# The last stage of a fused layer: u evicted bank by bank, products moved ahead of the LoRA and gate steps, result stored in quarters

## The reference, cut to what matters

```python
x = x + s4_conv(paged_attention(x))          # the convolution runs along the 512 features
X = x                                        # "x1" in the kernel
z = X @ W2.T + b2 + 2.0 * (X @ lA[ids]) @ lB[ids].T              # cond2: linear plus LoRA
result = z @ W.T + b                                             # the last layer
q, k = z @ Wq.T, z @ Wk.T                                        # 8 experts of 32
w = softmax(sum(q * k over the 32) / sqrt(32))                   # the gate
combined = sum_e w[e] * (z @ A[e].T) @ Bm[e].T
out = X + result + combined
```

## Time and profile before

| | |
|---|---|
| median of 3 runs | 1333.55 us (1330.68 to 1333.7) |
| the profiled execution | 1330.66 us |
| its span | 1328.8 us |
| PE busy | 1252.7 us, 94% |
| mean granted TensorE clock | 0.976 |
| last stage of half 0, from the end of `Wo` to the next half | 606.3 to 679.3 us of the span |
| last stage of half 1, from the end of `Wo` to the end | 1256.4 to 1328.8 us of the span |

### The profile page before, as it was taken

The page is one execution under the profiler, slowest core; times in us unless marked ns, Lnnn a source line. Parts: engine busy times, 40 slices in busy tenths (PEclk is TensorE's granted clock), DMA queues, the critical chain, the costliest instruction groups (busy, mean ns, idle before and its releaser), DMA issues.

```text
span 1328.8 us, 28755 instructions
## 1 busy us (share of the span) xinstructions
PE 1252.7 (94%) x7378; PEld 1044.1 (79%) x7378; DVE 812.1 (61%) x1724; ACT 810.9 (61%) x2256; POOL 768.2 (58%) x901
## 2 busy tenths in 40 slices
PE   6899969999999998998989999699999999999998
PEld 4678859989999986765657788598989899978756
DVE  5976546776767666852147766376776767665412
ACT  3676658888888873431135766478888888744320
POOL 3444348888888864533033434388888888754310
PEclk9999979999999998998989999799999999999999
DMA  7241388888888825305134322888888888234200
GB/s 242 88 135 63 123 235 221 234 244 241 233 229 237 233 64 171 124 1 191 37 108 127 114 93 87 243 226 236 239 241 231 234 233 236 76 114 151 101 0 32
DMA packets 148104, 214.82 MB, mean 162 GB/s; under 512 B 25844, under 2 KB 120374, under 8 KB 142006
## 3 DMA queue, kind: packets, MB, share of 16 engines
q1 hardware_dynamic: 128646, 202.75, 52.3%
q10 hardware_dynamic: 18576, 9.05, 2.5%
q0 software_dynamic: 800, 2.10, 0.5%
HBM read 203.33 MB, written 10.49 MB: 161 GB/s over the span
## 4 chain that ended last, share of the span: by engine, by line
PE 81%; DVE 6%; issue 3%; DMA 3%; ACT 3%; ACTq 2%; POOL 1%; SPq 0%; DVEq 0%; POOLq 0%; PEldq 0%
PE PS L1031 17%; PE PS L999 9%; PE PS L930 4%; PE PS L926 4%; PE PS L922 4%; PE PS L1040 4%; PE PS L1090 3%; PE PS L1081 3%; PE PS L1087 3%; PE PS L966 2%; PE PS L968 2%; PE PS L1139 2%; PE PS L901 2%; PE PS L984 2%; PE PS L988 2%
## 5 line engine op out<-in xcount | busy, mean ns | idle before, releaser
L574 POOL TENSOR_TENSOR kv_parts<-kv,k_hi 128x544 fp32r<-128x544 f32 x192 | 258.6, 1347 | 41.7 <-ACT k_hi L765 40.2
L1031 PE MATMUL PS<-probT,kv 128*128 128x128 f32 x2048 | 270.5, 275 | 0.0
L527 POOL TENSOR_TENSOR ring_parts<-ring,kv_parts 128x512 fp32r<-128x512 f32 x96 | 128.9, 1349 | 229.8 <-ACT kv_parts L641 229.8
L1031 PEld LDWEIGHTS PS<-probT,kv 128*128 128x128 f32 x2048 | 249.0, 192 | 0.1
L1461 DVE COPY probT<-PS 128x512 f32<-128x512 f32 x256 | 175.6, 686 | 3.1 <-PE PS L999 3.1
L804 ACT ACTIVATE ring<-ring,smin 128x544 f32<-128x544 f32 x192 | 143.8, 749 | 37.8 <-DVE smin L1455 36.8
L1455 DVE CUSTOM_DVE_ANT_0 ring<-PS,mask,rq 128x544 f32<-128x544 f32 x192 | 150.1, 782 | 21.8 <-PE PS L989 13.5
L765 ACT ACTIVATE k_hi<-kv 128x544 fp32r<-128x544 f32 x192 | 126.0, 657 | 52.6 <-PE PS L989 48.7
L605 POOL TENSOR_TENSOR ring_parts<-ring,kv_parts 128x512 fp32r<-128x512 f32 x64 | 89.3, 1400 | 104.5 <-ACT kv_parts L844 104.4
L562 POOL TENSOR_SCALAR ring<-ring,rinv 128x512 f32<-128x512 f32 x192 | 133.3, 694 | 0.0
L922 PE MATMUL PS<-kv_parts 128*128 128x512 f32 x384 | 115.1, 417 | 18.4 <-ACT kv_parts L641 15.7
(11 more groups left out here) (212 smaller groups left out, 2711.2 us busy)
## 6 DMA issues: line engine op xcount, KB each, us to landing
kv<-in_kpages SPq DMA_DIRECT2D x512, 128.0 KB, 2.3
kv<-in_vpages SPq DMA_DIRECT2D x496, 128.0 KB, 3.2
ring<-in_w SPq DMA_DIRECT2D x46, 1024.0 KB, 4.9
kv<-in_xT SPq DMA_DIRECT2D x4, 1024.0 KB, 8.8
v_new<-kv ACTq DMA_DIRECT2D x64, 64.0 KB, 2.9
k_new<-kv ACTq DMA_DIRECT2D x16, 256.0 KB, 2.3
kv<-k_new SPq DMA_DIRECT2D x32, 128.0 KB, 2.6
kv<-v_new SPq DMA_DIRECT2D x32, 128.0 KB, 2.4
```

Of the source, the lines that this page charges most:

```text
L574: nc.gpsimd.tensor_tensor(kbuf_lo(par)[:, :, g, :], kbuf(par)[:, :, g, :], k_hi[:, e % 2, :].rearrange("p (j t) -> p j t", t=PSIZE), ALU.s ...
L1031: mm = nc.tensor.matmul(PS[:, at:at + D], vbuf(bpar)[:, c, gg * D:(gg + 1) * D], probT[:, g % 2, c * P:(c + 1) * P], start=(c == 0 and a = ...
```

## The change

All of it lies in the last stage. In the last head of `Wo` the banks are done from 3 down to 0, each raises `u_ready`, and ACT and DVE copy each bank as it is final. The copies go to `mask` and `probT`, buffers of the attention, since `qo` is still being read. The convolution waits for each chunk of u by itself. cond2's products for o = 0 stand ahead of LoRA A, those for o = 1 ahead of LoRA B. The last layer's products with chunk 0 of z, for all four o, stand ahead of the gate. Behind the gate come the rest of o = 0 and 1, the transposes, the rest of o = 2, the combination for o = 0 to 2, the rest of o = 3, and its combination. The output of a half is stored by four DMAs of 256 KB, one for each chunk.

```diff
-        uT = part(0, 2048).rearrange("p (c n) -> p c n", c=KC)
+        uT = [mask[:, 0, 0:LC], mask[:, 1, 0:LC], probT[:, 0, :], probT[:, 1, :]]
...
-                sp.wait_ge(out_ready, KC * (h + 2))
-                sp.dma_start(out_d[:, ds(h * HT, HT)].rearrange("(c p) t -> p c t", p=P), outT)\
-                    .then_inc(out_done, 16)
+                for o in range(KC):
+                    sp.wait_ge(out_ready, KC * (h + 1) + o + 1)
+                    sp.dma_start(out_d[o * P:(o + 1) * P, ds(h * HT, HT)], outT[:, o, :]).then_inc(out_done, 16)
...
                 for c in (3, 2):
-                    act.wait_ge(u_ready, 4 * h + 4)
-                    nc.scalar.activation(uT[:, c, :], bank(c), ACT.Copy).then_inc(u_act, 1)
-
+                    act.wait_ge(u_ready, 4 * h + KC - c)
+                    nc.scalar.activation(uT[c], bank(c), ACT.Copy).then_inc(u_act, 1)
+
+                act.wait_ge(u_ready, 4 * h + 4)
...
-                    for c in range(KC):
+                    order = range(KC) if head < HQ - 1 else range(KC - 1, -1, -1)
+                    for k, c in enumerate(order):
...
-                        if a == 3 and c == 3:
+                        if head == HQ - 1:
+                            mm.then_inc(u_ready, 1)
+                        elif a == 3 and k == 3:
                             mm.then_inc(w_free, 1)
-                        elif head == HQ - 1:
-                            mm.then_inc(u_ready, 1)
...
-                pe.wait_ge(w_free, h * (BLOCKS // 2) + 8 + SLOTS)
-                pe.sem_inc(u_ready, 1)
-
-
-                pe.wait_ge(u_act, 2 * h + 2)
+                pe.wait_ge(u_ready, 4 * h + 4)
+                pe.sem_inc(w_free, 1)
+
+
                 pe.wait_ge(w_in[0], h * 96 + 96)
                 for t in range(KC):
                     for c in range(KC - 1, KC - 2 - t, -1):
+                        if t == 0:
+                            pe.wait_ge(u_act, 2 * h + 1)
+                        if t == 1 and c == 2:
+                            pe.wait_ge(u_act, 2 * h + 2)
...
+                def cond(o):
+
+                    for c in range(KC):
+                        pe.wait_ge(x1_ready, 4 * h + c + 1)
+                        nc.tensor.matmul(bank(1 + o), slot(1)[:, c, o * P:(o + 1) * P], x1T[:, c, :],
+                                         start=(c == 0), stop=False)
...
+                pe.wait_ge(w_in[1], h * 96 + 96)
+                pe.wait_ge(u_dve, 2 * h + 2)
+                cond(0)
                 pe.wait_ge(lora_packed, NGRP * (h + 1))
                 pe.wait_ge(last_in, 48 * (h + 1))
-                pe.wait_ge(x1_ready, 4 * h + 4)
-                pe.wait_ge(u_dve, 2 * h + 2)
...
+                cond(1)
+                pe.wait_ge(interm, h + 1)
+                cond_lora(0)
+                cond_lora(1)
+                for o in range(2, KC):
+                    cond(o)
+                    cond_lora(o)
...
+                def last(o, c):
+
+                    os = slice(o * P, (o + 1) * P)
+                    nc.tensor.matmul(bank(o), last_hi[:, 1, c, os], z_hi[:, c, :], start=(c == 0), stop=False)
+                    nc.tensor.matmul(bank(o), last_hi[:, 1, c, os], z_lo[:, c, :], start=False, stop=False)
+                    return nc.tensor.matmul(bank(o), slot_lo(3)[:, c, os], z_hi[:, c, :], start=False, stop=False)
+
+
+                pe.wait_ge(llo_ready, (h + 1) * (2 * KC))
+                pe.wait_ge(zhi_ready, 4 * h + 1)
+                pe.wait_ge(zlo_ready, 4 * h + 1)
+                pe.wait_ge(z_read, 4 * h + 3)
+                for o in range(KC):
+                    last(o, 0)
 
                 pe.wait_ge(z_read, 4 * h + 4)
...
+                for o in range(2):
+                    for c in range(1, KC):
+                        last(o, c)
                 pe.wait_ge(wh_ready, h + 1)
                 for m in range(TILES):
                     mm = nc.tensor.transpose(bank(4)[:, m * P:(m + 1) * P], wh[:, m * P:(m + 1) * P], ident)
                 mm.then_inc(wht_ready, 1)
+                for c in range(1, KC):
+                    last(2, c)
                 pe.wait_ge(wht_read, h + 1)
-                for o in range(KC):
-                    nc.tensor.matmul(bank(o), bmT[:, o * P:(o + 1) * P], whT, start=False, stop=True)\
-                        .then_inc(o_ready, 1)
+                for o in range(3):
+                    combine(o)
+                for c in range(1, KC):
+                    mm = last(3, c)
+                mm.then_inc(w_free, 1)
+                combine(3)
...
                 for c in (1, 0):
-                    dve.wait_ge(u_ready, 4 * h + 4)
-                    V.tensor_copy(uT[:, c, :], bank(c)).then_inc(u_dve, 1)
+                    dve.wait_ge(u_ready, 4 * h + KC - c)
+                    V.tensor_copy(uT[c], bank(c)).then_inc(u_dve, 1)
```

More of the change, by code:

```diff
@@ L1117, in _ @@
                             pe.wait_ge(u_dve, 2 * h + 2)
-                        mm = nc.tensor.matmul(bank(4 + t), slot(0)[:, c, t * P:(t + 1) * P], uT[:, c, :],
+                        mm = nc.tensor.matmul(bank(4 + t), slot(0)[:, c, t * P:(t + 1) * P], uT[c],
                                               start=(c == KC - 1), stop=(c == KC - 1 - t))
@@ L1122, in _, with cond_lora @@
                 pe.sem_inc(w_free, 1)
+                def cond(o):
[3 more added lines that the diff above has]
+                                         start=(c == 0), stop=False)
+                def cond_lora(o):
+                    for r in range(NGRP):
+                        mm = nc.tensor.matmul(PS[:, 512 * (1 + o) + 256 * r:512 * (1 + o) + 256 * (r + 1)],
+                                              lB[:, r, o * P:(o + 1) * P], inter[:, 256 * r:256 * (r + 1)],
+                                              start=False, stop=(r == NGRP - 1))
+                    mm.then_inc(z_ready, 1)
+                pe.wait_ge(w_in[1], h * 96 + 96)
+                pe.wait_ge(u_dve, 2 * h + 2)
+                cond(0)
                 pe.wait_ge(lora_packed, NGRP * (h + 1))
                 pe.wait_ge(last_in, 48 * (h + 1))
-                pe.wait_ge(x1_ready, 4 * h + 4)
-                pe.wait_ge(u_dve, 2 * h + 2)
                 for r in range(NGRP):
@@ L1154, in _ @@
                 pe.wait_ge(zlo_ready, 4 * h + 4)
-                pe.wait_ge(llo_ready, h * (2 * KC) + KC)
                 for m in range(TILES):
@@ L1173, in _, with combine @@
                 pe.sem_inc(w_free, 1)
-                pe.wait_ge(llo_ready, (h + 1) * (2 * KC))
-                for o in range(KC):
-                    os = slice(o * P, (o + 1) * P)
-                    for c in range(KC):
-                        nc.tensor.matmul(bank(o), last_hi[:, 1, c, os], z_hi[:, c, :], start=(c == 0), stop=False)
-                        nc.tensor.matmul(bank(o), last_hi[:, 1, c, os], z_lo[:, c, :], start=False, stop=False)
-                        mm = nc.tensor.matmul(bank(o), slot_lo(3)[:, c, os], z_hi[:, c, :],
-                                              start=False, stop=False)
-                mm.then_inc(w_free, 1)
+                def combine(o):
+                    nc.tensor.matmul(bank(o), bmT[:, o * P:(o + 1) * P], whT, start=False, stop=True)\
+                        .then_inc(o_ready, 1)
+                for o in range(2):
+                    for c in range(1, KC):
+                        last(o, c)
                 pe.wait_ge(wh_ready, h + 1)
```

19 lines of the change are left out of this document (4 added, 15 removed).

## The result

The changed kernel takes 1321.55 us (median of 4 runs, 1318.64 to 1323.01), the kernel before 1332.88 us beside it (4 runs, 1330.68 to 1333.7). The ratio is 0.9915, with a 95% interval of 0.9894 to 0.9936: faster by 11.3 us, or 0.85%. The profiled executions took 1330.66 and 1318.64 us, both at the fast end of their four; their spans are 1328.8 and 1316.9 us.

The account below looks back on a forecast made before the run. PE was taken as the bound, so only its holes, slow stretches and the tail counted: 1.2 + 1.4 + 4.5 + 3.2 + 1.4 + 1.9 = 13.6 us, 1330.66 to 1317.1 profiled, median 1320.0, range 1316 to 1325.

Parts of the forecast that it names:

- u, bank by bank: End of `Wo`: copying each bank once final cuts PE's wait of 1.34 us; half 1 gains 1.2 us, half 0 nothing.
- cond2 ahead of LoRA A: Ahead of LoRA A: cond2's products for o = 0 hide the 0.83 us wait for x1; both halves gain 1.4 us together.
- The gate's hole: Ahead of the gate: twelve early last-layer products replace holes of 2.40 and 2.37 us; gain 4.5 us, with 0.8 us cover.
- a restart costs 0.15 us: Wherever a hole closes: PE's restart after waiting on its own last product was priced at 0.15 us, taken from the gate's end.
- The slow stretch: Gate's first twelve products: with no hole ahead they start at full clock, 2.82 instead of 4.41 us; 3.2 us for both halves.
- Behind the gate: Transposes and combination: `wh` is ready in time and the 0.69 us copy of `whT` is hidden; 1.4 us for both halves.
- The store: Program's end: the last DMA carries 256 KB instead of 1 MB, landing in 2.3 instead of 4.2 us; gain 1.9 us.
- the rival of the queueing quarters: Final store: four DMAs run in a row, the last landing 4.5 us after issue; 1322.2 us in all, chance 0.05.
- The turn: Start of the next half: POOL's subtractions move ahead of DVE's four; between 0.8 us lost and 1.1 gained, taken as 0.
- The clock fell at no gate: Rival at the gate: the granted clock still dips without the hole, so 3.2 us are missing; 1323.2 us, chance 0.12.
- half 0's gain reached the end: Rival at the turn to half 1: half 0's share of 5.2 us is lost there; 1325.2 us, chance 0.05.
- no wait was late: Rival in the last stage: a wait called old (z's last chunk or `wh`) is late, up to 6 us return; 1326, chance 0.05.

Follow-up runs that it names:

- experiment 8: The change with ACT's and DVE's copies of u waiting for all of `Wo`, the convolution still starting behind ACT's first copy alone; 1324.48 us.
- experiment 3: Experiment 1 with cond2's first products also put back behind LoRA A; 1325.0 us.
- experiment 11: The change with PE's waits for its own last product, ahead of telling SP that a slot is free, moved a few products later at four places a half; 1318.36 us.
- experiment 5: The kernel before with twelve additional last-layer products ahead of the gate, their results thrown away; 1331.91 us, 0.9999 of before.
- experiment 10: The kernel before with only the edit of experiment 9, POOL's second four subtractions waiting for DVE's four; 1331.52 us.
- experiment 1: The change with the twelve early last-layer products put back behind the gate; 1325.65 us, 0.9951 of before.
- experiment 2: The same kernel as experiment 1, the change without early last-layer products, run once more; 1328.63 us.
- experiment 4: The change with only six early last-layer products (o = 0 and 1) ahead of the gate, the other six behind it; 1321.14 us.
- experiment 6: The change with one DMA of 1 MB for a half's output in place of four; 1325.36 us.
- experiment 7: The change with the combinations of all four o behind all last-layer products, so the four stores are issued 0.88 us apart; 1319.62 us.
- experiment 9: The change with POOL's second four subtractions at the start of a half waiting for DVE's four; 1317.39 us, 0.9892 of before.
- experiment 12: The change with the edits of experiment 9 and experiment 11 together; 1314.66 us, 0.9867 of before.

## Why the prediction was right, point by point

The forecast was 1320.0 us in the range 1316 to 1325, and 1321.55 was measured; the sum was 13.6 us, and the profiled executions differ by 12.0, the medians by 11.3. The time came closer than the gain by luck: the kernel before took 0.7 us less beside the change than the median that I had started from.

- **u, bank by bank.** The mechanism was right, the size not: 1.34 - 0.38 = 0.96 us instead of 1.2, with no gain in half 0, as forecast. The term was mis-sized through the restart (below). Its working, that the copy is done before PE gets there, holds, but experiment 8 shows that the finer wait gives most of it.
- **cond2 ahead of LoRA A.** 0.53 us a half, 1.1 together, instead of 1.4; experiment 3 measured 0.52. Same cause.
- **The gate's hole.** Nothing waits at the gate, as forecast; z's last chunk was ready 1.1 us ahead, 0.8 was forecast. Each half gains 2.40 - 0.42 or 2.37 - 0.42, together 3.9 us instead of 4.5.
- **The step that failed: "a restart costs 0.15 us".** I took it from one place, the end of the gate, and put it in wherever a hole closed. It measured 0.30 to 0.42 us, so these three terms gave 1.1 us less. The idle column isn't even the whole price: with the four waits on PE's own last product gone, half 1 got 2.2 us shorter, 0.55 for each (experiment 11). Behind such a wait the first product also comes slower: 0.31 us to the next one instead of 0.23.
- **The slow stretch.** The term came out whole: both gates run at 1.00, and from z's end on, each half gained 4.4 us (4.42 and 4.44), against 4.5 in the sum (2.25 for the hole, 1.6 for the clock, 0.69 for `whT`). That the clock pays was shown by experiment 5. The forecast took it for granted that the hole always costs its 1.6 us, from two gates that were both slow; that is partly luck. It did in seven of ten gates behind a hole of 2.26 to 2.40 us (both of before and both of experiment 10; half 0 of experiments 1 to 3) and not in the three of half 1 in experiments 1 to 3. Of the 18 gates of the change and of experiments 4 to 9, 11 and 12, behind no hole or one of 0.22 us, none was slow.
- **Behind the gate.** `wh` and `whT` are hidden, 1.4 us, right.
- **The store.** 1.96 us against 1.9; experiment 6 gives 1.9 back. The Trainium skill's page "DMA: Bandwidth & Descriptors", section "Anatomy of one DMA", fits DMAs issued by GpSimd, which I didn't say in the prediction; these are issued by SyncE. Its fit would have put the last quarter at 2.6 us, as an estimate. It lands 2.0 us after its issue, and what doesn't grow with size is about 1.3 us here (the estimate in experiment 7), not the section's 2.0. Where the measurement and the fit differ, the measurement decides. The parts that don't grow with size overlap (experiment 7), so cutting up costs nothing at the end of this program: the rival of the queueing quarters is ruled out there.
- **The turn.** I said that POOL's work moves ahead of DVE's four and bounded this between 0.8 us lost and 1.1 gained, and took 0. It lost 1.03. The step behind the bound was wrong: I reckoned that one of DVE's four would change its duration. I also misread the row: its 10.65 us are seven of POOL's subtractions, and all eight took 12.07. ACT came 8.6 us earlier in the run, PE's first product 5.4, and POOL's eight (11.24 us, until 682.08) ran beside nearly all of DVE's four (until 682.63). With POOL out of the way the four take 2.50 us, so this contention costs 4 us. Most of it was there before the change, where the four took 5.93: the change itself added 0.56 us of it. Of the 1.03 us that PE lost, 0.44 come while it waits for DVE's four, and 0.59 behind them, where the low clock lasts longer: PE's second group of four behind them took 1.91 us, where before it took 1.42. The Trainium skill's page "SBUF — State Buffer", section "SBUF: two separate sides", describes an exclusive lock between a GpSimd instruction that reads SBUF and a VectorE instruction with two SBUF inputs, which is what these subtractions are. The rows fit it, though they don't tell a lock from any other way of being in each other's way: about 0.62 us apiece alone (2.50 / 4), 1.62 beside POOL (6.49 / 4).
- **The rivals.** The clock fell at no gate; the quarters don't queue; half 0's gain reached the end but for the 1.0 us at the turn; no wait was late. Of the signs, "holes of at most 0.2 us" and a convolution within 0.3 us of `Wo` failed with the restart (0.30 to 0.42 us).

The account: 1.1 us less through restarts and 1.0 through the turn take the 13.6 us to 11.5. The shorter slow stretch and DMA wait of half 0's convolution add 0.9, the scatter of the long stretches takes 0.8, which makes 11.6 of the 12.0 us between the profiled executions; 0.4 us are small differences that I didn't follow up.

**What stays open.** Why half 1's gate kept its clock three times behind a hole of 2.26 us, where 2.37 and 2.40 us were followed by the fall. It isn't cond2's place (experiment 3). What differs in half 1 between the two groups is the hole at u (0.38 against 1.34 us), 0.11 to 0.14 us in the length of the hole itself, and the moment at which the hole comes. In the seven slow gates the clock falls 0.3 to 1.1 us behind the gate's first product, and half 0 is always among them. The gate of half 1 follows that of half 0 after 644.8 and 645.0 us where both were slow (before, experiment 10), and after 643.4, 643.4 and 643.7 us where only half 0's was (experiments 1 to 3). So the moment is a rival as good as the others; no run parts them. If the fall in half 1 could have been had without the early products, 1.6 us of the clock's 3.2 can't be put down to them alone: experiments 1 and 2 leave it so.

## What to carry to other kernels

Fill a hole of TensorE of over 2 us with products that have to run anyway and whose inputs are ready: the hole's length is gained once, and here at seven gates of ten 1.6 us of clock with it; six products, leaving 0.22 us, were enough for the clock. Price a wait of TensorE on its own last product at about 0.55 us, the mean of four here, and not at its idle column, and put such a wait, when it only tells others that a buffer is free, a few products later. And when a change makes one engine early, look at whom it now runs beside: at the turn 1 us was lost when GpSimd started earlier, and letting VectorE go first gave 4 to 5.

## What the runs showed of the hardware

- Subtractions of two engines, both from SBUF, slow each other: four of VectorE's took 2.50 us with GpSimd idle and 6.49 beside GpSimd's (experiment 9); four of GpSimd's took 5.00 us ahead of VectorE's (experiment 9) and 5.88 with VectorE's beside them in part (experiment 10).
- A DMA of 256 KB from SBUF to DRAM landed 2.0 us after its issue at the end of the program, one of 1 MB 4.2 us (before and experiment 6; 5.0 and 5.2 in half 0, beside a weight load); four quarters issued 0.88 us apart landed as fast as four spread over 5 us.
- Behind a hole of over 2 us the granted clock didn't fall at once: in experiment 2, half 0, the gate's first four products took 1.00 us at a granted clock of 1.00, and the last seven 2.98 us, 0.43 apiece, at 0.50, the level of 1.2 GHz.

```profile
649.72:650.72 1.00, 1.00 (x4) 0.83 (x5) 0.00 (x0) 0.00 (x0) 0.00 (x0) 1.00 0.95 401
651.06:654.04 2.98, 2.98 (x8) 2.34 (x7) 0.00 (x0) 0.00 (x0) 0.00 (x0) 0.50 0.21 88
```
